# Per-head q, k and V moved by DMA in place of TensorE transposes, in a two-layer conditioned transformer block

## The chip, the cores and the metric

The program runs on one core of one Trainium2 chip. The metric is the device time of one execution in microseconds (us), lower is better. A core has five engines that run their own instruction streams and meet only at semaphores: TensorE (PE; PEld is its weight load), VectorE (DVE), ScalarE (ACT), GpSimd (POOL) and SyncE (SP), which here only issues DMAs. Sixteen DMA engines move the data. TensorE reads SBUF and writes PSUM; PSUM has 8 banks of 128 x 512 fp32.

## The reference

Inputs: x is 2 x 1024 x 288, a condition vector per batch is 288 long. Two layers follow each other.

```
U = qr(P).Q                              # 288 x 64
R = expm(skew(silu(c) W^T + b))          # one 64 x 64 rotation per batch
x = x + (x U R - x U) U^T

ada = silu(c) @ ada_w + ada_b            # six vectors of 288 per batch
h   = modulate(layernorm(x))
q, k, v = h @ qkv_w + qkv_b              # 16 heads of 18 for each token
a   = softmax(q k^T / sqrt(18)) v        # over the heads of one token, see below
x   = x + gate * (a @ proj_w + proj_b)
x   = x + gate * mlp(modulate(layernorm(x)))     # 288 -> 1152 -> gelu -> 288
```

The einsum of the attention is `nthd,ntkd->nthk`: the softmax runs over the 16 heads of one token, so every token has its own 16 x 16 score matrix. The kernel computes 8 tokens at once in one 128 x 128 matmul (8 tokens x 16 heads on each side) and masks the pairs of different tokens with extra operand rows.

## The kernel before, in words

All work is on 16 tiles of 128 tokens, handled as 4 chunks of 4 tiles. The order is written out by hand in five blocks, one per engine, with explicit semaphores. Nothing is scheduled by a planner.

1. From 0 to 111 us: the QR and the matrix exponential, a long chain of small fp32 matmuls. The weights come in and POOL splits them into fp16 halves.
2. From 111 to 217 us, the **qkv stage**: the rotation of x is finished (`delta`, `rotated`), the layernormed chunk is turned (`turn`, on PE), scaled and split into a high and a low fp16 half (`turn_out` on ACT, `split` on DVE), and multiplied with the qkv weights. The multiplication goes in 48 **slots** (`gu` 0 to 47): slots 3t, 3t+1 and 3t+2 make q, k and v of one tile. Two tiles are a **pair** (8 pairs), so a pair has 6 slots. One slot is 7 matmuls (`qkv`), a copy out of PSUM that makes the high half (`high`, ACT) and a second one that makes the low half (`low`, DVE).
3. Attention reads q and k with the head dimension on partitions. So in the qkv stage there are also **jobs**: `job` is 8 matmuls against an identity (L787 for q and k, L764 through `v_columns` for v), and `job_out` copies 128 x 512 out of PSUM on ACT (L1101, L1099) into `QKT` and `VT`. A pair has 4 jobs for q, 4 for k and 4 for v. The v jobs of pairs 4 to 7 are done later, inside the attention (`v_late`, `v_late_out`). The jobs of a slot lag the pair's products by 7 slots, so eight q and k jobs of the last pair come behind slot 47.
4. From slot 24 on, `maxima` (PE, L751) and `maximum` (DVE, L1373) compute the negative row maximum of each of the 32 **units** (64 tokens each, two 128 x 512 banks). Units 0 to 15 are done in the qkv stage, two of every three slots, units 16 to 31 in the first half of the attention. The maxima are turned by PE (`max_turn`) and written by small DMAs into one row of `QKT` (`max_row`).
5. From 217 to 282 us, the **attention**, 32 units in a software pipeline: `scores` (PE, L843), `exponentials` (ACT, L1129), `values` (PE, L880). Four units are a **round** (one pair): in each round V is regrouped by 32 small matmuls (`v_groups`, L866), copied by ACT (`v_out`, L1138) into `VG`, the output is copied out (`values_out`), turned back (`turn_values`, L896) and divided by the row sum (`normalise`, DVE). Scores of units up to 18 use one pair of banks; later ones alternate between two, since the maxima are then finished.
6. From 282 us: projection, then the MLP, which ends the program.

The PSUM banks in the qkv stage are 2 and 5 for the products (`UB`), 6 and 7 for the jobs (`CB`), 3 and 4 for the maxima, 0 and 1 for `turn`. The product of slot gu waits until the low half of slot gu - 2 is out.

The functions that the change touches follow with the line numbers of the profile.

## Time and profile before

| | us |
|---|---|
| median of 3 runs | 427.33 |
| lowest, highest | 426.06, 427.52 |
| span of the profiled execution | 422.3 |
| qkv stage | 111.0 to 217.3 |
| attention | 217.3 to 281.8 |
| projection | 281.8 to 306.6 |
| MLP | 306.6 to 422.3 |

The profile has the span of the profiled execution and no time of its own for it. The timed runs are 3.8 to 5.2 us longer than the span, and this part lies outside what the engines' records show. The stage borders are read from the first and last instruction of the lines named above. Busy time of PE is not PE at its peak: matmuls overlap, and a line's mean duration (294 ns for one of the seven matmuls of a slot) is more than twice the distance between two of them.

### The profile page before, as it was taken

How to read it: one execution, taken by the hardware profiler on the slowest of the kernel's cores; microseconds unless marked ns; L12 is line 12 of the kernel's file. 1: busy time of each engine (PE TensorE's matmuls, PEld its weight loads, DVE VectorE, ACT ScalarE, POOL GpSimd, SP SyncE). 2: the span in 40 equal slices, each digit the busy share in tenths (PEclk: the TensorE clock that was granted, in tenths of full speed). 3: DMA queues.
4: the chain of work that ended last, by engine and by line, in shares of the span. 5: the costliest groups of instructions: out<-in, count | busy, mean ns of one | idle time of the engine just before them, and what ended most of it. 6: DMA issues, size and time to landing. Idle time of an engine off the chain costs nothing.

```text
span 422.3 us, 11278 instructions
## 1 busy us (share of the span) xinstructions
PE 397.1 (94%) x4547; PEld 256.5 (61%) x4547; DVE 291.1 (69%) x793; ACT 231.8 (55%) x485; POOL 115.9 (27%) x137
## 2 busy tenths in 40 slices
PE   8999999999989899899978898889999999999996
PEld 4656555666545566666646565558755566666675
DVE  2688875677689856667757766666899776746452
ACT  3356334433257899997786785665775342422100
POOL 5039999981008700000000000005420010101040
PEclk9999989999989999999999999999999999999999
DMA  6999000000000000000000000000000000000011
GB/s 166 305 316 271 24 4 2 12 7 2 2 0 2 2 2 3 2 2 5 2 4 3 5 4 4 4 2 2 0 2 1 16 28 16 23 20 16 29 43 42
DMA packets 7926, 14.68 MB, mean 35 GB/s; under 512 B 2555, under 2 KB 6239, under 8 KB 7748
## 3 DMA queue, kind: packets, MB, share of 16 engines
q1 hardware_dynamic: 7874, 13.96, 11.0%
q8 instruction: 36, 0.59, 0.6%
q14 instruction: 16, 0.13, 0.1%
HBM read 11.52 MB, written 2.38 MB: 33 GB/s over the span
## 4 chain that ended last, share of the span: by engine, by line
PE 71%; DVE 14%; ACT 10%; issue 4%; ACTq 0%; DVEq 0%
PE psum L957 13%; PE psum L973 13%; PE psum L517 9%; PE psum L803 6%; ACT scratch L1068 3%; PE psum L787 2%; PE psum L880 2%; PE psum L617 2%; DVE MX L1373 2%; ACT big L1101 2%; PE psum L934 2%; PE psum L629 2%; PE psum L751 2%; PE psum L573 2%; PE psum L608 2%
## 5 line engine op out<-in xcount | busy, mean ns | idle before, releaser
L957 PE MATMUL psum<-scratch,W 128*128 128x512 f16 (+1 forms) x252 | 57.9, 379 | 0.0
L973 PE MATMUL psum<-W,big 128*128 128x288 f16 x432 | 55.1, 286 | 0.0
L506 POOL TENSOR_TENSOR X<-X,big 128x288 f32<-128x288 f32 x16 | 13.0, 826 | 150.0 <-ACT big L1174 149.7
L803 PE MATMUL psum<-WQ,scratch 128*128 128x288 f16 (+1 forms) x336 | 50.5, 294 | 2.8 <-DVE scratch L1368 1.9
L1199 ACT ACTIVATE big<-psum 128x512 f32<-128x512 f32 x36 | 21.3, 597 | 57.3 <-PE psum L957 52.3
L973 PEld LDWEIGHTS psum<-W,big 128*128 128x128 f16 x432 | 42.2, 98 | 12.9
L1373 DVE TENSOR_REDUCE MX<-psum 128x8 f32<-128x1024 f32 x32 | 39.0, 1220 | 11.4 <-PE psum L751 11.0
L517 PE MATMUL psum<-ident 128*32 128x192 f32 (+3 forms) x142 | 43.8, 393 | 0.0
L1129 ACT ACTIVATE big<-psum 128x1024 f32<-128x1024 f32 x32 | 32.9, 1032 | 15.0 <-PE psum L843 14.7
L957 PEld LDWEIGHTS psum<-scratch,W 128*128 128x128 f16 (+1 forms) x252 | 24.6, 98 | 25.6
L803 PEld LDWEIGHTS psum<-WQ,scratch 128*128 128x128 f16 (+1 forms) x336 | 30.6, 100 | 14.8 <-DVE scratch L1368 2.4
L1068 ACT ACTIVATE scratch<-psum,MOD 128x512 f32<-128x512 f32 (+3 forms) x48 | 34.3, 774 | 5.3 <-PE psum L728 4.0
L511 POOL TENSOR_TENSOR X<-X,scratch 128x288 f32<-128x288 f32 x16 | 13.5, 856 | 83.6 <-DVE big L1529 83.6
L1101 ACT CAST big<-psum 128x512 f16<-128x512 f32 x64 | 34.5, 597 | 0.1
L1027 ACT ACTIVATE scratch<-psum,scratch 64x65 f32<-64x65 f32 x63 | 19.5, 309 | 26.8 <-DVE scratch L1271 26.7
L1527 DVE TENSOR_SCALAR big<-big 128x512 f16<-128x512 f32 x36 | 15.6, 435 | 26.8 <-ACT big L1199 26.8
L1024 ACT ACTIVATE scratch<-scratch 64x1 f32<-64x1 f32 x63 | 12.8, 202 | 26.7 <-DVE scratch L1266 26.1
L1529 DVE SCALAR_TENSOR_TENSOR big<-big 128x512 f16<-128x512 f32 x36 | 26.3, 732 | 1.2
L1368 DVE TENSOR_TENSOR scratch<-scratch 128x512 f16<-128x512 f32 (+1 forms) x24 | 17.5, 731 | 11.1 <-ACT scratch L1068 10.9
L787 PE MATMUL psum<-ident,stage 128*64 128x128 f16 x512 | 22.2, 223 | 3.2 <-ACT big L1101 2.4
L1085 ACT ACTIVATE stage<-psum 128x576 f16<-128x576 f32 x32 | 21.0, 655 | 7.1 <-PE psum L803 6.5
L880 PE MATMUL psum<-big,scratch 128*32 128x128 f32 x512 | 22.4, 287 | 1.7 <-ACT big L1129 1.1
(221 smaller groups left out, 770.5 us busy)
## 6 DMA issues: line engine op xcount, KB each, us to landing
X<-in_x_dram SPq DMA_DIRECT2D x4, 576.0 KB, 14.8
out_dram<-big SPq DMA_DIRECT2D x16, 144.0 KB, 1.7
big<-in_L_cond_W_dram SPq DMA_DIRECT2D x1, 2268.0 KB
big<-in_L_cond_ada_w_dram SPq DMA_DIRECT2D x2, 864.0 KB, 18.2
stage<-in_L_cond_fc_w_dram SPq DMA_DIRECT2D x1, 1296.0 KB, 18.9
big<-in_L_cond_fc_w_dram SPq DMA_DIRECT2D x1, 1152.0 KB
stage<-in_L_cond_qkv_w_dram SPq DMA_DIRECT2D x1, 864.0 KB
big<-in_L_cond_fc_w_dram SPq DMA_DIRECT2D x3, 144.0 KB
```

The lines of the kernel that those rows point to most:

```text
L517: pe.matmul(out[:, 0:cols], left, left[:, 0:1].broadcast_to([P, cols]), start=True, stop=True)
L787: mm = pe.matmul(out[R * c_:R * c_ + R, P * hh:P * hh + P], HQ[:, 2 * (pr % 2) + c_, w, 4 * q + hh, :], ident16[:, :], start=True, stop=True)
L803: mm = pe.matmul(UB[gu % 2][:, 0:D], HT[0:r, n % 2, a_, P * a:P * a + P], WQ[0:r, w_, D * w:D * w + D], start=(p_ == 0), stop=(p_ == 6))
L880: mm = pe.matmul(PO[c_][32 * g:32 * g + 32, P * q:P * q + P], VG[:, w % 2, c_, 4 * q + g, :], E[:, s_ % 2, c_, P * g:P * g + P], start=Tru ...
L957: mm = pe.matmul(FB[idx % 3], W1[0:r, w_, P * m:P * m + P], HT[0:r, n % 2, a_, :], start=(p_ == 0), stop=(p_ == 6))
L973: mm = pe.matmul(YB[t % 2][:, 0:D], g[:, a_, f, cols], W2[:, w_, f, :], start=(f == 0 and a_ + w_ == 0), stop=(f == NF - 1 and w_ == 1))
L1068: act.activation(dst, src, ACT.Identity, scale=MOD[0:rows, 2 * l + 1, b, batch:batch + 1], bias=MOD[0:rows, 2 * l, b, batch:batch + 1]).th ...
L1101: act.copy(columns(QKT[pr // 4][:, w, :], 16 * (pr % 4), q), src.rearrange("p (h v m) -> p h v m", h=4, v=16)).then_inc(col_done, 1)
L1129: act.activation(E[:, s_ % 2, :, :], psum[:, 3:5, :] if s_ > PAIRED and s_ % 2 else psum[:, 0:2, :], ACT.Exp, scale=DH ** -0.5 / (QSCALE * ...
L1199: act.activation(G32[:, idx % 2, :], FB[idx % 3], ACT.Gelu, scale=1.0 / (FINE * FINE)).then_inc(gelu_sb, 1)
L1373: dve.tensor_reduce(MX[:, n, :].rearrange("p (c g) -> p c g", c=2)[:, :, 4 * u:4 * u + 4], psum[:, 3:5, :].rearrange("p a (g c) -> p a g c ...
L1529: dve.scalar_tensor_tensor(out=GT[c_ % 2][:, 1, m, :], in0=G32[:, idx % 2, :], scalar=FINE, in1=GT[c_ % 2][:, 0, m, :], op0=ALU.mult, op1= ...
```

## The change

- **q and k.** The high and low halves of a pair are written by ACT and DVE into `HQ`, now laid out so that one row holds, for each head, the 64 columns of both tiles (e) side by side. One DMA transpose for q and one for k (`turn_heads`, 128 x 2048 fp16 each) writes `QKT`. Two pairs of `HQ` are held. The 64 q and k jobs of PE and ACT are gone. The order of tokens and heads inside a pair's columns changes, and `operand` reads them with a stride; `order` is dropped, and `TOK` is built to suit.
- **V.** ACT scales v out of PSUM in fp32 (`SV`, 4 buffers). A DMA stores it in DRAM (`store_values`), 16 heads of 18 values per token, 72 bytes each at 16 places. Two DMAs per pair (`spread_values`) read it back in the grouped form `VG`, again in runs of 72 bytes. `VG` has 6 buffers; pairs 6 and 7 are read in the attention. `v_columns`, `v_groups`, `v_out`, `v_late`, `v_late_out` and the low half of v are gone.
- **Products** use three banks (`UB`), and the product of slot gu waits for slot gu - 3.
- **Maxima.** ACT scales `MX` into `MRT` without a turn on PE; four DMAs in place of two write a quarter of the pairs' row.
- **POOL** clears `VG` (128 x 4096 before the folding of the projection weights, 128 x 2048 after the last split); DVE did a smaller clear before.
- New waits: `high` of pair p waits for both transposes of pair p - 2, the v copy for the store four tiles earlier, `maxima` of a pair's first unit for its transposes, `values` for the reads of its pair.

```diff
-        HQ = stage[:, 0:4096].bitcast(F16).rearrange("p (a w h c) -> p a w h c", a=TPC, w=2, h=H)
+        SV = scratch[:, o:o + 4 * D].rearrange("p (a d) -> p a d", a=4)
+        HQ = stage[:, 0:4096].bitcast(F16).rearrange("p (a w h e c) -> p a w h e c", a=2, w=2, h=H, e=2)
...
-        UB, CB = [bank[2], bank[5]], [bank[6], bank[7]]
+        UB = [bank[2], bank[5], bank[6]]
...
+            def store_values(pr, c_):
+                k = 2 * pr + c_
+                sp.wait_ge(v_copied, k + 1)
+                sp.dma_start(values_d[pr, c_].rearrange("h p d -> p h d"), SV[:, k % 4, :].rearrange("p (h d) -> p h d", h=H)).then_inc(v_stored[k % 4], 16)
+
+            def turn_heads(pr, w):
+                if pr == NCH and w == 0:
+                    sp.wait_ge(x_rot, NT)
+                    sp.wait_ge(folded, 2 * B)
+                sp.wait_ge(qk_low, lows(6 * pr + 3 + w))
+                dst = QKT[pr // NCH][:, w, 16 * P * (pr % NCH):16 * P * (pr % NCH + 1)]
+                sp.dma_start_transpose(dst.rearrange("p (h t) -> p h t", h=H),
+                                       HQ[:, pr % 2, w].rearrange("p h e c -> p (h e c)")).then_inc(qk_in[pr], 16)
+
+            def spread_values(w):
+                for c_ in range(2):
+                    sp.wait_ge(v_stored[(2 * w + c_) % 4], 16 * (w // 2 + 1))
+                if w < 6:
+                    sp.wait_ge(vg_clear, 2 if w < 4 else 4)
+                else:
+                    sp.wait_ge(pv_ready, 4 * (w - 6) + 4)
+                for c_ in range(2):
+                    src = bass.AP(tensor=values_d.tensor, offset=values_d.offset + P * D * (2 * w + c_), ap=[[D, P], [DH, 16], [1, DH]])
+                    sp.dma_start(VG[w % 6][:, c_, :, 0:DH], src).then_inc(v_in[w], 16)
...
+            for pr in range(2 * NCH):
+                store_values(pr, 0)
+                turn_heads(pr, 0)
+                turn_heads(pr, 1)
+                store_values(pr, 1)
+                if 1 <= pr < 5:
+                    spread_values(pr - 1)
+                if pr == 6:
+                    max_row(0)
+            spread_values(4)
+            spread_values(5)
+            for n in range(1, 3):
+                max_row(n)
+                spread_values(5 + n)
+            max_row(3)
...
-                if gu >= 2:
-                    pe.wait_ge(qk_low, gu - 1)
+                if gu >= 3 and w == 2:
+                    pe.wait_ge(v_copied, gu // 3)
+                elif gu >= 3:
+                    pe.wait_ge(qk_low, lows(gu - 3))
...
-                for i in slots.get(gu, ()):
-                    job(i)
...
+                if w == 2:
+                    k = gu // 3
+                    if k >= 4:
+                        act.wait_ge(v_stored[k % 4], 16 * (k // 4))
+                    act.mul(SV[:, k % 4, :], UB[gu % 3][:, 0:D], 1.0 / (FINE * FINE)).then_inc(v_copied, 1)
+                    return
...
+                if pr >= 2:
+                    act.wait_ge(qk_in[pr - 2], 32)
```

Three places show what moves. On PE, the last slots of the qkv stage and the start of the attention, before. L803 is a slot's product, L787 are q and k jobs, L751 maxima, L757 the turn of the maxima, L843 scores, L866 the regrouping of V.

```order
L751 MATMUL psum<-big 128x128 x8
L803 MATMUL psum<-WQ,scratch 128x288 x7
L787 MATMUL psum<-ident,stage 64x128 x16
L751 MATMUL psum<-big 128x128 x8
L803 MATMUL psum<-WQ,scratch 128x288 x7
L757 MATMUL psum<-ident,MX 64x128
L787 MATMUL psum<-ident,stage 64x128 x64
L843 MATMUL psum<-big 128x128 x8
L866 MATMUL psum<-SELV,big 128x18 x32
```

The same place in the changed kernel (L800 is the product, L782 the maxima, L838 the scores, L852 the values).

```order
L782 MATMUL psum<-big 128x128 x8
L800 MATMUL psum<-WQ,scratch 128x288 x7
L782 MATMUL psum<-big 128x128 x8
L800 MATMUL psum<-WQ,scratch 128x288 x7
L838 MATMUL psum<-big 128x128 x8
L782 MATMUL psum<-big 128x128 x8
L838 MATMUL psum<-big 128x128 x8
```

The jobs between the slots, the 64 matmuls of eight jobs behind the last slot, and the regrouping of V have left PE; the scores follow the last product directly.

On ACT at the same place, before. L1080 and L1085 are `high` for v and for q or k, L1101 the job copies, L1092 the scaled maxima, L1129 the exponentials.

```order
L1101 CAST big<-psum 128x4x16x8 x2
L1085 ACTIVATE stage<-psum 128x16x36
L1101 CAST big<-psum 128x4x16x8 x2
L1080 ACTIVATE scratch<-psum 128x16x18
L1092 ACTIVATE MRT<-psum 64x128
L1101 CAST big<-psum 128x4x16x8 x8
L1129 ACTIVATE big<-psum 128x1024
```

And in the changed kernel (L1037 is the v copy, L1045 `high` for q or k, L1052 the scaled maxima, L1080 the exponentials).

```order
L1045 ACTIVATE stage<-psum 128x16x2x18
L1045 ACTIVATE stage<-psum 128x16x36
L1037 ACTIVATE scratch<-psum 128x288
L1052 ACTIVATE MRT<-MX 128x64
L1080 ACTIVATE big<-psum 128x1024 x5
```

ACT loses every job copy between the slots and the eight behind the last one.

On SP, the changed kernel's transfers of pair 4 and of pairs 6 and 7 (L377 stores V, L385 transposes q and k, L397 reads V, L405 writes the row of maxima); SP had two small transfers of maxima in this stretch before.

```order
L377 DMA value_rows<-scratch 128x16x18 [waits v_copied]
L385 DMA_TRANSPOSE big<-stage 128x16x128 [waits qk_low,folded,x_rot]
L385 DMA_TRANSPOSE big<-stage 128x16x128 [waits qk_low]
L377 DMA value_rows<-scratch 128x16x18 [waits v_copied]
L397 DMA big<-value_rows 128x16x18 [waits vg_clear,v_stored3,v_stored2]
L397 DMA big<-value_rows 128x16x18
...
L405 DMA big<-MRT 1x128x16 [waits mr_ready]
L405 DMA big<-MRT 1x128x16 x3
L377 DMA value_rows<-scratch 128x16x18 [waits v_copied]
L385 DMA_TRANSPOSE big<-stage 128x16x128 [waits qk_low] x2
```

All of it is in one queue and in order, so a transfer that waits holds back those behind it.

## Rows read from the trace of the kernel before

**Rows 1.** The page: the span.

```profile
span 422.3 us, 11278 instructions
```

**Rows 2.** Windows of qkv stage: stretch, length, busy us PE, PEld, DVE, ACT, POOL; clock.

```profile
136.20:169.60 33.40, 31.53 (x437) 21.23 (x438) 23.34 (x65) 30.62 (x61) 8.85 (x10) 1.00 0.01 2
169.60:217.30 47.70, 43.30 (x657) 29.83 (x655) 32.76 (x45) 40.57 (x79) 0.00 (x0) 1.00 0.01 3
```

**Rows 3.** Timeline, slot 24 and a slot near 188 us: start, us, engine, line.

```profile
168.05 1.03 PE L803 MATMUL psum<-WQ,scratch 128*128 128x288 f16 x7
...
187.97 1.03 PE L803 MATMUL psum<-WQ,scratch 128*128 128x288 f16 x7
188.94 0.64 PE L787 MATMUL psum<-ident,stage 128*64 128x128 f16 x16
189.05 0.65 ACT L1085 ACTIVATE stage<-psum 128x576 f16<-128x576 f32 x1
189.73 0.46 DVE L1414 SCALAR_TENSOR_TENSOR stage<-psum,stage 128x288 f16<-128x288 f32 x1 [1.31 <-ACT stage L1085]
```

**Rows 4.** Timeline: the last slot, what follows it, and the first scores.

```profile
211.08 0.40 PE L751 MATMUL psum<-big 62*128 62x128 f16 x8
211.30 0.46 DVE L1414 SCALAR_TENSOR_TENSOR stage<-psum,stage 128x288 f16<-128x288 f32 x1 [0.27 <-ACT stage L1085]
211.41 1.03 PE L803 MATMUL psum<-WQ,scratch 128*128 128x288 f16 x7
211.67 1.22 DVE L1373 TENSOR_REDUCE MX<-psum 128x8 f32<-128x1024 f32 x1
...
213.69 4.36 ACT L1101 CAST big<-psum 128x512 f16<-128x512 f32 x8
...
217.35 0.40 PE L843 MATMUL psum<-big 63*128 63x128 f16 x8
```

**Rows 5.** The page's costliest groups: the split of a turned block on DVE.

```profile
L1368 DVE TENSOR_TENSOR scratch<-scratch 128x512 f16<-128x512 f32 (+1 forms) x24 | 17.5, 731 | 11.1 <-ACT scratch L1068 10.9
```

**Rows 6.** Timeline of POOL ahead of the folding of the projection weights.

```profile
110.55 1.10 POOL L484 MEMSET scratch<- 32x512 f16 x2 [14.17 <-PE psum L685]
127.52 1.40 POOL L490 TENSOR_TENSOR big<-big 128x576 f32<-128x576 f32 x1 [15.87 <-ACT big L993]
```

**Rows 7.** DMA alone, 60 to 64 us, a store in 64 B runs: packets, MB, share of 16 engines.

```profile
q1 hardware_dynamic: 266, 0.02, 4.3%
```

**Rows 8.** DMA alone, 194 to 198 us, two 8 KB transfers in 256 B runs.

```profile
q1 hardware_dynamic: 96, 0.02, 2.1%
```

**Rows 9.** DMA alone, 340 to 346 us, one 144 KB store in 1152 B runs.

```profile
q1 hardware_dynamic: 144, 0.15, 6.9%
```

**Rows 10.** Timeline of DVE in the attention's first half: reductions of units 24 to 28.

```profile
234.23 1.23 DVE L1373 TENSOR_REDUCE MX<-psum 128x8 f32<-128x1024 f32 x1 [0.58 <-PE psum L751]
235.95 1.23 DVE L1373 TENSOR_REDUCE MX<-psum 128x8 f32<-128x1024 f32 x1 [0.50 <-PE psum L751]
237.90 1.23 DVE L1373 TENSOR_REDUCE MX<-psum 128x8 f32<-128x1024 f32 x1 [0.72 <-PE psum L751]
240.38 1.22 DVE L1373 TENSOR_REDUCE MX<-psum 128x8 f32<-128x1024 f32 x1
242.18 1.23 DVE L1373 TENSOR_REDUCE MX<-psum 128x8 f32<-128x1024 f32 x1 [0.58 <-PE psum L751]
```

**Rows 11.** Timeline of PE in the second half: scores of units 24, 28 and 31.

```profile
265.21 0.40 PE L843 MATMUL psum<-big 63*128 63x128 f16 x8
...
272.89 0.40 PE L843 MATMUL psum<-big 63*128 63x128 f16 x8
...
277.56 0.40 PE L843 MATMUL psum<-big 63*128 63x128 f16 x8
```

**Rows 12.** The chain of waits: the first slot's seven matmuls.

```profile
121.13 1.88 PE psum L803 x7
```

**Rows 13.** Window of the first slots, columns as in rows 2.

```profile
121.00:124.00 3.00, 2.87 (x13) 1.76 (x14) 2.42 (x7) 1.33 (x3) 0.00 (x0) 0.50 0.00 0
```

More of the change, by code:

```diff
@@ L143, in build @@
         T32 = scratch[:, o:o + 2 * CH].rearrange("p (a n) -> p a n", a=2)
-        VG = scratch[:, 0:4 * CH].rearrange("p (a c g d) -> p a c g d", a=2, c=2, g=16)
+        VGS = [big[:, 8192 + 2 * CH * i:8192 + 2 * CH * (i + 1)] for i in range(4)] + [scratch[:, 2 * CH * i:2 * CH * (i + 1)] for i in range(2)]
+        VG = [v.rearrange("p (c g d) -> p c g d", c=2, g=16) for v in VGS]
         o += 2 * CH
@@ L201, in build @@
         att_const = sem("att_const")
-        col_ready, col_done = sem("col_ready"), sem("col_done")
-        vcol_ready, vcol_done = sem("vcol_ready"), sem("vcol_done")
-        mr_psum, mr_ready = sem("mr_psum"), sem("mr_ready")
+        qk_in = [sem(f"qk_in{i}") for i in range(2 * NCH)]
+        v_copied = sem("v_copied")
+        v_stored = [sem(f"v_stored{i}") for i in range(4)]
+        v_in = [sem(f"v_in{i}") for i in range(2 * NCH)]
+        mr_ready = sem("mr_ready")
         max_in = [sem(f"max_in{i}") for i in range(NCH)]
@@ L297, in build @@
         MROWS = HALVES + 8
-        jobs, slots = [], {}
-        for pr in range(2 * NCH):
-            for k in range(12 if pr < NCH else 8):
-                slots.setdefault(6 * pr + 7 + k // 2, []).append(len(jobs))
-                jobs.append((pr, k // 4, k % 4))
-            for n in (0, 1):
-                if pr == (4, 6)[n]:
-                    slots.setdefault((36, 48)[n], []).append(len(jobs))
-                    jobs.append(("max", n))
-        JOB = {j: i for i, j in enumerate(jobs)}
         AHEAD = {24 + 3 * s_ // 2: s_ for s_ in range(16)}
         LATER = {st: 1 for st in range(16)}
-        ROWS_LATER, ROWS_BANK = {8: 2, 16: 3}, {8: VB[0], 16: MXB[0]}
+        ROWS_EARLY = {36: 0, 3 * 4 * NCH: 1}
+        ROWS_LATER = {8: 2, 16: 3}
         PAIRED = 18
@@ L314, in build @@
         EXP_TABLE_AT = 2 * NQ + 1
-        NSLOT = 6 * 2 * NCH + 7 + 4
-        assert max(slots) < NSLOT
+        NSLOT = NQ * NCH + 1
         def unit(gu):
@@ L393, in _ @@
-            for n in range(NCH):
+                    for k in range(2):
+                        at = 16 * P * (2 * (n % 2) + k)
+                        row = QKT[n // 2][R * c_ + MROWS:R * c_ + MROWS + 1, 0, at:at + 16 * P]
+                        sp.dma_start(row, MRT[:, n % 2, 32 * c_ + 16 * k:32 * c_ + 16 * k + 16]).then_inc(max_in[n], 16)
+            for pr in range(2 * NCH):
[7 more added lines that the diff above has]
+                    max_row(0)
@@ L441, in _ @@
                                      pattern=[[0, 1]], channel_multiplier=1))
-            chain(pool.tensor_copy(SELV[:, :], ident[:, 0:DH]))
-            for j in (DH, R, R + DH):
-                chain(pool.tensor_tensor(SELV[:, :], SELV[:, :], ident[:, j:j + DH], ALU.add))
             for src, dst, n, s_ in ((SWQ, WQ, 3 * D, in_wq), (SW1, W1, MLP, in_w1)):
@@ L726, in turn @@
                             pe.wait_ge(xn_ready, modulated(n) + 1)
-                        if n < NCH:
-                            mm = pe.transpose(f[0:rows, cols], XN[:, n % 2, j, r0:r0 + rows], order[:, :])
-                            continue
                         if not attended:
@@ L743, in maxima @@
                 if s_ % 4 == 0:
-                    pe.wait_ge(col_done, JOB[(s_ // 4, 1, 3)] + 1)
+                    pe.wait_ge(qk_in[s_ // 4], 32)
                 if s_ == 0:
@@ L1115, in _ @@
                     norm_root(1)
-                for i in slots.get(gu, ()):
-                    job_out(i)
+                if gu in ROWS_EARLY:
+                    rows_out(ROWS_EARLY[gu])
                 if GATE_AT <= gu < GATE_AT + 4:
@@ L1163, in _ @@
                         values_out(st // 4 - 1)
-                    if st % 4 < 2 and st // 4 + 1 == 4:
-                        for q in range(2 * (st % 4), 2 * (st % 4) + 2):
-                            v_late_out(st // 4 + 1, q)
-                if st % 4 == 3 and st // 4 + 1 < UNITS // 4:
-                    v_out(st // 4 + 1)
             def product_out(t):
@@ L1454, in normalise @@
                     dve.wait_ge(weights, 5)
+                    for pr in range(2 * NCH):
+                        dve.wait_ge(qk_in[pr], 32)
                 for c_ in range(2):
@@ L1483, in _ @@
                     values_out(st // 4 - 1)
-                if st % 4 < 2 and 4 < st // 4 + 1 < UNITS // 4:
-                    for q in range(2 * (st % 4), 2 * (st % 4) + 2):
-                        v_late_out(st // 4 + 1, q)
                 if st >= 4 and st % 4 == 2:
```

211 lines of the change are left out of this document (55 added, 156 removed).

## The prediction

> **What bounds the kernel now.** I read the windows by stage first, since the share of a whole span mixes stages, then the timeline inside the two stages that the change touches, then the DMA queue. The change leaves everything before 121 us and after 282 us alone, so the question is how long the 161 us between them become.
>
> In the qkv stage two windows matter [rows 2]. From 136.2 to 169.6 us (slots 8 to 24) ACT is busy 30.6 of 33.4 us and PE 31.5; DVE only 23.3. From 169.6 to 217.3 us ACT is busy 40.6 of 47.7 us, PE 43.3, DVE 32.8. The jobs fill PE and ACT. A slot's seven matmuls occupy PE for 0.97 us (187.97 to 188.94), a pair of jobs is 0.64 us more, and the job copies keep ACT so that the next thing waits [rows 3]. Behind the last slot (211.41 us) come 4.36 us of job copies, and the first scores start only at 217.35 [rows 4]. In the attention's first half the reductions of the maxima follow each other on DVE at 1.72 to 2.48 us [rows 10]; in the second half a round of four units takes 7.68 us (265.21 to 272.89) with V's matmuls and copies in it, while the last round, which has none, does three units in 4.67 us [rows 11].
>
> **Slots 8 to 24.** The jobs leave: 17 slots x 0.64 us = 10.9 us of PE, so PE keeps 31.5 - 10.9 = 20.6 us. ACT loses its job copies and drops far below. DVE loses the low half of v in 5 or 6 slots, 2.5 us by 0.46 us each [rows 3], and keeps 20.8 us [rows 2]. PE and DVE are now equal. Two engines that hand work to each other never both stay full, so I add 3 us to the floor of 20.8 and take 23.9 us for 33.4: **9.5 us less**. The ends are 12.6 (the floor) and 5.
>
> **Slots 24 to 47.** Here a round of three slots (q, k, v) with two maxima is a chain. From rows 3 and 4: product to next PE work 0.97 us, product start to `high` 1.08, `high` start to `low` 0.68, `low` holds DVE 0.37 before a maximum can start, a maximum is 1.22, maxima hold PE 0.33 (211.08 to 211.41), PE to DVE 0.45. Start the q product at 0. Its low half is on DVE at 1.76; the first maximum runs 2.13 to 3.35. The k product starts at 1.30, but the second maxima wait on PE for that first maximum until 3.40, so v's product starts at 3.73 and the next q at 4.70. A round is 4.70 us, bound by the pair PE-DVE; ACT has air. 23 slots are 7.67 rounds, 36.0 us, and three turned blocks with a 0.73 us split each [rows 5] add about 1 us each: 39.0 us. Before it took 43.4 us (168.05 to 211.41) [rows 3, 4]: **4.4 us less**. The ends are 0 and 9 (PE alone, 3 x 0.97 + 2 x 0.33 a round).
>
> **Behind slot 47.** The scores follow the product: 217.35 - 211.41 - 0.97 = **5.0 us less** [rows 4]. The clear of `VG` goes to POOL, which stood idle for 15.87 us before the folding [rows 6]: free. If it weren't, the transposes of pair 4 would wait for the folding, at slot 28, 15 us later. With these three terms the scores start 18.9 us earlier. The row of maxima goes out by four transfers in place of two, but it is asked for at slot 41 and at the last slot, and read at the first and at the ninth unit; 8 KB transfers land within 2 us of queue and engine time unless the queue is full, which is the case below.
>
> **Attention.** First half: a round of reductions is 7.95 us now (234.23 to 242.18). Without V's steps the interval 1.95 becomes 1.72, and the normalising step keeps its 2.48 [rows 10]: 7.64, times four rounds, 1.2 us less, and 0.8 for the first regrouping that stood ahead of the first maxima. Second half: the last round, with its fourth unit at the mean of the three, is 6.2 us against 7.68 [rows 11]; three rounds have V's work: 4.4 us less. Together **6.4 us less** (ends 2 and 12).
>
> **What it adds: 48 transfers on one queue.** No row shows a transpose. Prices per transfer come from packets. The store in 64 B runs took 4.3% of 16 engines x 4 us = 2.75 us for 266 packets, 10.3 ns each [rows 7]; V's 72 B runs are the nearest thing, 2048 of them over 16 engines: 1.3 us a store or a read. Transfers from SBUF to SBUF in 256 B runs took 1.34 us of engine time for 16 KB [rows 8]; a transpose reads 512 KB, 32 times as much, 43 us over 16 engines: 2.7 us. The ends: at the rate of 1152 B runs (6.6 us for 144 KB) it is 1.5 us [rows 9]; if it moves 64 B pieces it is 8192 x 10.3 ns / 16 = 5.3 us; if each piece written is 16 rows of one 2-byte column, 32 B, it is 10.5 us. I take 2.7, since those are the only SBUF to SBUF rows.
>
> Call the price of a transpose X. Pair 1 is ready at about 137 us. Pairs 1 to 4 put 2X + 5.2 us in the queue each (two transposes, two stores, two reads), pair 5 a store and two transposes before its `qk_in`, and 2 us is landing: done at 137 + 10X + 24.1 = 161.1 + 10X. Slot 42 needs it, and six slots (9.0 us) follow until the scores. So the DMA alone lets the scores start at 170.1 + 10X. At X = 2.7 this is 197.1; the engines give 217.35 - 18.9 = 198.5. The queue is just behind the engines' pace and costs nothing, but each further 0.1 us of X then costs 1 us. This is the thin place of the forecast. `high` of pair p + 2 is the waiting instruction; behind it on ACT stand the v copies and the scaling of the next chunk, and through them PE.
>
> The Trainium skill (DMA: Bandwidth & Descriptors, section Latency and other measured facts) gives 261 GB/s for a transpose with a non-contiguous middle dimension; by an estimate from that figure, 512 KB take 2.0 us, and the queue would be out of the way. The trace has no transpose to check it.
>
> **Sum.** Span 422.3 [rows 1] - 9.5 - 4.4 - 5.0 - 6.4 = 397.0 us. The page gives no time beside its span; the median of the runs, 427.3, lies 5.0 us above it. 397.0 + 5.0 = **402 us**, 6% less. Its own range is 391 to 412.
>
> **Rivals.**
>
> *The queue takes part of it.* X lies between 3.5 and 5.3 us. The scores then start at 205 to 223 us, and with 6.4 us from the attention the time is 409 to 427. For it: 64 B pieces are priced at 5.3. Against: nothing in the trace.
>
> *The queue turns it slower.* Transposes in 32 B pieces: X = 10.5. Scores start at 275.1, 57.8 us later than now; pair 7's transposes land 48.5 us after pair 5's, at 314.6, where unit 28's maxima want them at about 298, 16.5 us more; less 6.4: 427.3 + 57.8 + 16.5 - 6.4 = 495 us. It is decided by X alone: from 170.1 + 10X - 217.35 = 6.4, X = 5.4 us, the kernel is slower than before. The same holds at a smaller X if V's packets cost more than 10.3 ns: each ns more is 0.13 us on a transfer, 2.2 us over the 17 that stand between pair 1 and the transposes of pair 5. The place is ACT's wait for `qk_in`. For it: neither a transpose nor a run that scatters into DRAM at 72 B steps has been seen, and 64 B packets already move only 6 GB/s an engine against 23 for 1152 B [rows 7, 9].
>
> The Trainium skill states that against this change on the same page, section Specifications: below 512 B a DMA engine does read-modify-write and is off line rate. The trace agrees that short runs are slow; their price above includes it for aligned 64 B runs, not for 72 B ones.
>
> A second sentence there, in DMA Transpose, lets only one transposing stream run at a time; all transposes are on SP here, so it changes nothing.
>
> *TensorE falls to its lower clock.* PE is busy less: 3.57 of 4.70 us in a round. The first slots, behind a wait of PE, ran at a granted clock of 0.50, 1.2 GHz, one product taking 1.88 us for 0.97 [rows 12, 13]. If half of the eight rounds ran so, each with 3 x 0.91 us more on PE less the 1.1 us that PE has spare, it costs 4 x 1.6 = 6.5 us, 13 if all did: 408 to 415. Against it: the clock stayed at 1.00 through both windows of rows 2.
>
> *The gain is not there.* PE and DVE block each other in slots 8 to 47 as before; only the tail and the attention pay: 427.3 - 5.0 - 6.4 = 416.
>
> **How the numbers follow.** Forecast (391 to 412): 0.46. Queue takes part: 0.14. Queue turns it slower: 0.28, of which I hold half to be under 455, X being anywhere from 5.4 up. Clock: 0.06. Gain not there: 0.06. About 0.5% (2 us) is what a measurement here tells from no change. Faster by more: 0.46 + 0.06 + 0.06 and 0.11 of the second case, 0.69; within it 0.04; slower 0.27. The range for 8 in 10 starts at 390 (0.05 left below) and goes up to 462, leaving about 0.13 above.
>
> **What would show it.** Right: first scores near 198 us, last slot's product 1 us before them; a round of slots 24 to 47 near 4.7 us; ACT idle, DVE above 80% busy in slots 24 to 47; landing times of transposes under 6 us, the wait of ACT for `qk_in` near zero; rounds of 7.6 us in the attention's first half, 6.2 in the second. Wrong: ACT, and PE behind it, wait for transposes at the start of each pair, with a DMA share near 1 (engine-bound) or low (then SP's issue or the crossbar sets the pace, not packets); a granted clock of 0.5 between 140 and 197 us.

## The result, and the profile after

The changed kernel takes **460.8 us** (median of 4 runs, 454.3 to 472.8) against 427.3 us before: a ratio of 1.074, 95% interval 1.066 to 1.081. The forecast was 402 us with a range from 390 up to 462. The direction was wrong. The ratios, here and below, leave out executions in a slower state (here the one of 472.8 us, which is also the profiled one), while the medians take in all.

The page's span is 471.0 us [rows 1]. In this one execution the stage before the first product ran 13 us longer than before (134.48 for 121.13 us), though the change leaves it alone; the other three have spans of 452 to 459. So stages are compared from the first product on. Timeline of PE after: start, us, engine, line; in square brackets the idle time before, and what ended it. The lines are the first slot, the last slot, the first scores, and the first product of the projection.

```profile
134.48 0.91 PE L800 MATMUL psum<-WQ,scratch 128*128 128x288 f16 x6 [1.89 <-DVE scratch L1297]
...
227.48 1.03 PE L800 MATMUL psum<-WQ,scratch 128*128 128x288 f16 x7
...
232.84 1.16 PE L838 MATMUL psum<-big 63*128 63x128 f16 x8 [4.32 <-DMA big<-MRT]
...
334.78 3.62 PE L892 MATMUL psum<-WP,scratch 128*128 128x288 f16 x28
```

From first product to first scores it is 98.4 us, where before took 96.2 [rows 4, 12] and the forecast was 77.4. From first scores to the projection it is 101.9 us, where before took 68.7 (217.35 to 286.09) and the forecast was 62.3. So 2 us were lost in the stage that should have paid 19, and 33 in the stage that should have paid 6. The scores do not follow the last product directly either: they start 5.4 us behind it (227.48 to 232.84), of which PE waits 4.32 us for the DMA that writes the first row of maxima from `MRT` into `QKT`.

What fills the attention is seen in its timeline after (same columns). It answers to [rows 10, 11].

```profile
241.44 1.17 PE L838 MATMUL psum<-big 63*128 63x128 f16 x8
242.43 1.14 PE L782 MATMUL psum<-big 62*128 62x128 f16 x8
242.65 1.02 ACT L1080 ACTIVATE big<-psum 128x1024 f32<-128x1024 f32 x1 [2.04 <-PE psum L838]
243.49 1.08 PE L852 MATMUL psum<-big 128*32 128x128 f32 x16
244.50 1.17 PE L838 MATMUL psum<-big 63*128 63x128 f16 x8
```

A unit comes every 3.06 us, and by the records PE never pauses in it. Eight matmuls of 128 columns, scores or maxima, occupy PE for 1.0 us where they took 0.33 before. ACT waits for PE. The groups by line say it for the whole stretch. Of PE before, 121 to 300 us (busy us, mean ns of one; L880 values, L751 maxima, L843 scores, L896 the turn of the values):

```profile
L880 PE MATMUL psum<-big,scratch 128*32 128x128 f32 x512 | 22.4, 287 | 1.7 <-ACT big L1129 1.1 <-ACT scratch L1146 0.3
L751 PE MATMUL psum<-big 62*128 62x128 f16 x256 | 13.1, 223 | 3.2 <-DVE MX L1373 3.1
L843 PE MATMUL psum<-big 63*128 63x128 f16 x256 | 12.9, 220 | 2.0 <-ACT big L1129 1.8
L896 PE MATMUL psum<-ident,scratch 128*128 128x128 f32 x64 | 8.7, 278 | 1.5 <-DVE scratch L1472 0.9 <-DVE big L1476 0.5
```

And after, 134 to 345 us:

```profile
L838 PE MATMUL psum<-big 63*128 63x128 f16 x256 | 37.1, 423 | 5.1 <-DMA big<-MRT 4.3 <-ACT big L1080 0.6
L782 PE MATMUL psum<-big 62*128 62x128 f16 x256 | 36.6, 418 | 8.9 <-DVE MX L1302 8.8
L852 PE MATMUL psum<-big 128*32 128x128 f32 x384 | 24.3, 399 | 0.1
L863 PE MATMUL psum<-ident,scratch 128*128 128x128 f32 x64 | 15.6, 426 | 0.9 <-DVE scratch L1398 0.9
```

Scores and maxima took about 24 us more each. Values and their turn, whose matmuls are the same, are slower too (399 ns for 287, 426 for 278), where the granted clock was low. Windows after (busy us of PE, PEld, DVE, ACT, POOL; then granted clock, DMA share, GB/s):

```profile
200.00:210.00 10.00, 8.65 (x55) 4.96 (x55) 4.46 (x6) 2.36 (x6) 0.00 (x0) 0.75 0.85 105
...
240.00:250.00 10.00, 10.00 (x110) 5.49 (x108) 3.95 (x4) 4.76 (x6) 0.00 (x0) 0.50 0.71 63
...
310.00:320.00 10.00, 10.00 (x106) 5.82 (x104) 2.72 (x6) 4.10 (x4) 0.00 (x0) 0.50 0.00 0
```

Before, the clock was 1.00 in the qkv stage from 136 us on [rows 2], and 0.94 and 1.00 in the two halves of the attention. Now it is 0.50, the 1.2 GHz level, in the two attention windows shown and 0.60 over the whole attention, though PE is busy for 99.8 of its 101.9 us. In the qkv stage the DMA share is near 1 (0.88 over the whole stage), and `high` on ACT waits four times for transposes (us in total, times, longest):

```profile
ACT stage L1045 <- DMA big<-stage: 8.7, 4, 4.5
```

Timeline of SP after, the transposes of pairs 1, 3, 4 and 5 (pairs count from 0):

```profile
155.47 5.36 SPq L385 DMA_TRANSPOSE big<-stage  x2
...
180.70 6.64 SPq L385 DMA_TRANSPOSE big<-stage  x2
...
194.91 5.26 SPq L385 DMA_TRANSPOSE big<-stage  x2
...
207.98 6.24 SPq L385 DMA_TRANSPOSE big<-stage  x2
```

Pairs follow each other at 13 us; my queue was 10.6 a pair (2 x 2.7 + 5.2). A store of V by itself, 139 to 142.5 us, answers to [rows 7]:

```profile
q1 hardware_dynamic: 2064, 0.15, 37.7%
```

37.7% of 16 engines x 3.5 us is 21.1 us for 2064 packets, 10.2 ns each, as priced. The error in the queue is not in the price of a store that has the queue to itself.

### The profile page after: what moved, and what is told of

It reads as the page before. It is cut to its first block, busy times and chain, and to the rows that moved or that the text cites. A ratio compares the mean times of both kernels' runs of the same rounds, so it can differ in the third digit from the quotient of the medians.

```text
span 471.0 us, 9049 instructions
## 1 busy us (share of the span) xinstructions
PE 442.5 (94%) x3519; PEld 271.4 (58%) x3519; DVE 276.0 (59%) x763; ACT 187.1 (40%) x385; POOL 120.1 (25%) x135
## 4 chain that ended last, share of the span: by engine, by line
PE 80%; DVE 8%; DMA 5%; ACT 4%; issue 2%; SPq 1%; ACTq 0%; DVEq 0%
PE psum L915 12%; PE psum L931 11%; PE psum L551 10%; PE psum L838 7%; PE psum L852 6%; PE psum L782 5%; PE psum L800 5%; DMA big<-stage 4%; PE psum L863 3%; PE psum L651 3%; PE psum L762 2%; PE psum L663 2%; PE psum L598 2%; PE psum L892 2%; ACT scratch L1026 2%
## 5 line engine op out<-in xcount | busy, mean ns | idle before, releaser
L800 PE MATMUL psum<-WQ,scratch 128*128 128x288 f16 (+1 forms) x336 | 53.9, 314 | 5.2 <-DVE stage L1342 2.9
L1080 ACT ACTIVATE big<-psum 128x1024 f32<-128x1024 f32 x32 | 32.8, 1025 | 56.5 <-PE psum L838 56.3
L551 PE MATMUL psum<-ident 128*32 128x192 f32 (+3 forms) x142 | 48.2, 427 | 0.0
L800 PEld LDWEIGHTS psum<-WQ,scratch 128*128 128x128 f16 (+1 forms) x336 | 33.6, 106 | 24.9 <-issue 10.0
L782 PE MATMUL psum<-big 62*128 62x128 f16 x256 | 36.6, 418 | 8.9 <-DVE MX L1302 8.8
L838 PE MATMUL psum<-big 63*128 63x128 f16 x256 | 37.1, 423 | 5.1 <-DMA big<-MRT 4.3
L782 PEld LDWEIGHTS psum<-big 62*128 62x128 f16 x256 | 17.9, 148 | 22.0 <-DVE MX L1302 11.7
L1045 ACT ACTIVATE stage<-psum 128x576 f16<-128x576 f32 x32 | 20.2, 648 | 22.6 <-PE psum L800 13.9
L838 PEld LDWEIGHTS psum<-big 63*128 63x128 f16 x256 | 16.5, 150 | 20.3 <-issue 13.8
L1342 DVE SCALAR_TENSOR_TENSOR stage<-psum,stage 128x288 f16<-128x288 f32 x32 | 14.4, 454 | 23.2 <-ACT stage L1045 23.0
```

The source lines that it names most:

```text
L551: pe.matmul(out[:, 0:cols], left, left[:, 0:1].broadcast_to([P, cols]), start=True, stop=True)
L782: mm = pe.matmul(MXB[c_][:, P * g:P * g + P], operand(s_, c_, 0, g, MROWS), operand(s_, c_, 1, g, MROWS), start=True, stop=True)
L800: mm = pe.matmul(UB[gu % 3][:, 0:D], HT[0:r, n % 2, a_, P * a:P * a + P], WQ[0:r, w_, D * w:D * w + D], start=(p_ == 0), stop=(p_ == 6))
L838: mm = pe.matmul(SB[s_ % 2 if s_ > PAIRED else 0][c_][:, P * g:P * g + P], operand(s_, c_, 1, g, MROWS + 1), operand(s_, c_, 0, g, MROWS + ...
L1045: act.mul(dst[:, :, 0:2, :] if w else dst[:, :, 0:3:2, :], src.unsqueeze(2).broadcast_to([P, H, 2, DH]), QSCALE / (FINE * FINE)).then_inc( ...
L1080: act.activation(E[:, s_ % 2, :, :], psum[:, 3:5, :] if s_ > PAIRED and s_ % 2 else psum[:, 0:2, :], ACT.Exp, scale=DH ** -0.5 / (QSCALE * ...
```

## The experiments

Three theories. *Stride*: `operand` now picks its 128 columns 16 apart, 32 B in fp16, and TensorE reads such an operand slowly. *Queue*: transposes and V's packets set the pace. *Clock*: TensorE simply falls to its lower clock, for waits or otherwise. A unit's scores, or its maxima, are eight matmuls of 128 columns, called "the eight" below; each matmul has a stationary operand (the weight load) and a moving one. The stage times of all runs stand in one table behind the experiments.

**e0_after.** No edit.

> The changed kernel again, for stage times beside the runs that follow. All theories: a span of 450 to 460 us, eight matmuls of scores or maxima about 1.1 us, qkv stage (first product to first scores) about 98 us, attention about 94 us.

Measured: 465.5 us (452.9 to 473.0, ratio to before 1.069, interval 1.056 to 1.082). The stages are those above within 0.5 us; 102.4 us for the attention is more than the 94 expected.

**e1_contig_both, e2_contig_weights, e3_contig_moving.**

```diff
-            return cols.rearrange("p (t v) -> p v t", v=16)[:, v]
+            return cols[:, P * v:P * v + P]        # both; in e2 the stationary operand alone, in e3 the moving one
```

> Leaves the computation of the reference: both operands of scores and maxima are 128 neighbouring columns of one head, in place of 16 heads x 8 tokens taken 16 columns apart; everything else as changed. Theory stride (the step of 32 B in the operands makes these matmuls slow): eight matmuls fall from 1.1 to 0.33 to 0.40 us, an attention round of four units from 12.3 to about 8 us, the time to 415 to 430 us. Theory queue (the transposes and V's transfers set the time): the matmuls may fall, but qkv stays at 98 us and the kernel above 445 us. Theory clock (TensorE runs at its lower clock there whatever it reads): eight matmuls stay above 0.75 us in the attention and the time above 445 us.

> Leaves the computation of the reference: only the stationary operand (the weight load) of scores and maxima is 128 neighbouring columns; the moving one keeps its step of 16 columns. Stride theory, if the weight load is what is slow: eight matmuls 0.4 us. If the moving side is: they stay at 1.1 us. If both are: 0.6 to 0.9 us. Queue and clock theories: time within 2% of the changed kernel.

> Leaves the computation of the reference: only the moving operand of scores and maxima is 128 neighbouring columns; the weights keep their step of 16 columns. Stride theory, if the moving side is what is slow: eight matmuls 0.4 us. If the weight load is: they stay near 1.1 us. If both: 0.6 to 0.9 us. Queue and clock theories: time within 2% of the changed kernel.

Measured: both 426.8 us (ratio 0.999, 0.995 to 1.004), weights alone 453.4 (1.064, 1.050 to 1.077), moving alone 429.3 (1.002, 0.998 to 1.007). The stride costs 34 us by the medians and 32 by the ratios, and it is the moving operand that is slow: by itself contiguous it gives back nearly all of it. Groups of PE with the moving operand contiguous (e3), 110 to 460 us:

```profile
L784 PE MATMUL psum<-big 62*128 62x128 f16 x256 | 16.6, 259 | 20.3 <-DVE MX L1304 20.2
L840 PE MATMUL psum<-big 63*128 63x128 f16 x256 | 16.2, 252 | 12.4 <-DMA big<-MRT 9.2 <-ACT big L1082 3.1
```

With the weights alone contiguous (e2):

```profile
L784 PE MATMUL psum<-big 62*128 62x128 f16 x256 | 35.1, 405 | 13.7 <-DVE MX L1304 13.7
L840 PE MATMUL psum<-big 63*128 63x128 f16 x256 | 34.8, 403 | 4.1 <-DMA big<-MRT 3.6 <-ACT big L1082 0.2
```

All the gain is in the attention (101.9 to 65.4 and 68.2 us). The qkv stage stays at 98 to 104 us, so something else sets it. The clock theory, by which the time would have stayed above 445 us whatever is read, falls here: the granted clock over the attention follows the moving operand, 0.60 in the changed kernel, 0.67 in e2, 0.89 in e3 and 0.93 in e1.

The 104.0 us of e1 need a correction. In its profiled execution the clock was 0.56 from 121 to 130 us and 0.71 from 130 to 140, where e3 had 0.82 and 1.00; the product of slot 5 starts 14.6 us behind the first in place of 10.3 (at 135.86 and 131.12 us). The profiled executions of f1, i1, f4 and h1 below have the same longer low stretch (0.50 to 0.55 until 130 us), those of e2, f2, i2, g1 and g2 have not (0.81 to 0.86). The edits do not explain it, since both groups have runs of the same form (f1 and i1 in one, f2 and i2 in the other). It puts about 4 us on the first stage time of e1, f1 and i1. The 109.8 of f4 and the 103.6 of h1 begin with such a stretch too.

**f4_before_strided.** The same edit the other way round, on the kernel before.

```diff
-            return QKT[b][R * c_:R * c_ + rows, w, P * (4 * u + g):P * (4 * u + g + 1)]
+            pr, v = divmod(4 * u + g, 16)
+            cols = QKT[b][R * c_:R * c_ + rows, w, 16 * P * pr:16 * P * (pr + 1)]
+            return cols.rearrange("p (t v) -> p v t", v=16)[:, v]
```

> The kernel before, no DMA transposes and V by PE; only operand reads scores' and maxima's columns 16 apart (the tokens are then mixed, so it leaves the computation of the reference). Theory stride: eight matmuls 1.1 us for 0.33 to 0.40, 64 groups by 0.7 us is 45 us of PE, a part of it hidden: 455 to 475 us. Theory that the transposes or their DMA traffic slow PE's reads of SBUF: no change, 425 to 432 us.

Measured: 476.3 us (1.112, 1.106 to 1.118), 48 us more by the ratio, at the upper end of what was expected. The stride alone does it, without transposes or V's transfers beside it. Its timeline of PE at a granted clock of 1.00 (L845 scores, L882 values):

```profile
307.43 1.12 PE L845 MATMUL psum<-big 63*128 63x128 f16 x8
308.49 0.64 PE L882 MATMUL psum<-big,scratch 128*32 128x128 f32 x16
```

The strided eight take 1.06 us to the next work at clock 1.00, and 0.99 to 1.07 at 0.50 (241.44 to 242.43 and 242.43 to 243.49 above for scores and maxima): their time hardly depends on the clock, while the values' goes from 0.57 to 1.01. And its window over 32 strided groups, columns as above:

```profile
229.60:286.50 56.90, 56.53 (x713) 34.78 (x711) 23.46 (x28) 25.16 (x37) 0.00 (x0) 0.61 0.01 2
```

PE is busy 56.5 of 56.9 us by the records, waits for other engines are nearly nil (0.4 us), and still the granted clock is 0.61. So the clock falls behind the strided matmuls, not behind waits, and the low clock is a second cost of the stride. The strided matmuls do not always bring it: from 300 to 312 us of the same run, with V's unstrided matmuls between the scores and PE busy for 11.7 of 12 us, it is 1.00. What decides between the two was not followed up.

**h1_steps.** The step measured by itself on the kernel before; the unit's number sets it.

```diff
+            k = (1, 2, 4, 8, 16, 0)[s_ % 6]
+            if k == 0 and moving:
+                return cols.rearrange("p (h v m) -> p v h m", h=16, v=16)[:, v]
+            k = max(k, 1)
+            return cols[:, 0:P * k].rearrange("p (t v) -> p v t", v=k)[:, v % k]
```

> A measurement on the kernel before (leaves the computation of the reference): the operands of scores and maxima of unit s are 128 columns at a step of 1, 2, 4, 8 or 16 columns (2 to 32 B) by s mod 6, and for s mod 6 = 5 the moving operand is 16 runs of 8 neighbouring columns, 256 B apart. If the step makes the read slow in proportion up to some size: eight matmuls 0.33 to 0.40 us at step 1 and 2, 0.6 at 4, 1.1 from 8 or 16 on. If any step over one column does it: 1.1 us at 2, 4, 8 and 16. Runs of 8: 0.4 us in either case, if reads within a run stay whole. Whole time between before's 427 and 465 us.

Measured (442.98 us, one run), scores of units 18 to 23 at clock 1.00: steps of 1, 2, 4, 8, 16 columns, then 16 runs of 8.

```profile
269.01 0.40 PE L849 MATMUL psum<-big 63*128 63x128 f16 x8
271.43 0.40 PE L849 MATMUL psum<-big 63*128 63x128 f16 x8
273.05 0.64 PE L849 MATMUL psum<-big 63*128 63x128 f16 x8
274.75 1.13 PE L849 MATMUL psum<-big 63*128 63x128 f16 x8
277.30 1.15 PE L849 MATMUL psum<-big 63*128 63x128 f16 x8
279.97 0.40 PE L849 MATMUL psum<-big 63*128 63x128 f16 x8
```

By these records steps of 2 and 4 B are free, 8 B costs 1.6 times, 16 B and 32 B the same 2.8 times, and runs of 16 B, 256 B apart, cost nothing. By the distance to the next work of PE it is 0.33, 0.33, 0.57, 1.06, 1.08 and 0.33 us. That is the first of the two expectations. In units with a step both operands have it; that the moving one carries the cost is known from e2 and e3, at 32 B. What fits all six is that the number of elements in one 16 B piece counts. The Trainium skill says so (Advanced Engine Details and Errata, section Memory Cachelines: SBUF has lines of 16 bytes, at least two hits on a line are needed, a new line at each access is penalised). The trace agrees with the penalty; at two hits a line (the step of 8 B) it is already 1.6 times, where by the Trainium skill it would be free. I had not weighed this in the prediction, and it speaks against the very layout that the change brings in.

**f1_few_values, f2_few_transposes, i1_few_stores, i2_few_reads.** All start from e1_contig_both, so that the stride is out, and take away traffic with the number of DMAs kept. The lines are shortened.

```diff
-  sp.dma_start(values_d[pr, c_].rearrange("h p d -> p h d"), SV[...].rearrange("p (h d) -> p h d", h=H))
+  sp.dma_start(values_d[pr, c_].rearrange("h p d -> p h d")[:, 0:1], SV[...].rearrange(...)[:, 0:1])   # f1, i1
-  src = bass.AP(..., ap=[[D, P], [DH, 16], [1, DH]])
-  sp.dma_start(VG[w % 6][:, c_, :, 0:DH], src)
+  src = bass.AP(..., ap=[[DH, P], [DH, 1], [1, DH]])                                                   # f1, i2
+  sp.dma_start(VG[w % 6][:, c_, 0:1, 0:DH], src)                                                       # f1, i2
+  src = bass.AP(..., ap=[[DH, P], [0, 16], [1, DH]])                                                   # i1
-  sp.dma_start_transpose(dst.rearrange("p (h t) -> p h t", h=H), HQ[:, pr % 2, w]...)
+  sp.dma_start_transpose(dst.rearrange("p (h t) -> p h t", h=H)[:, 0:2], HQ[:, pr % 2, w, 0:2]...)     # f2
-  return cols[:, P * v:P * v + P]
+  return cols[:, P * (v % 2):P * (v % 2) + P]                                                          # f2
```

> Leaves the computation of the reference, as e1_contig_both does (neighbouring columns), and of V only one head's 18 values per token are stored and read back: a sixteenth of V's packets, the number of DMAs unchanged. Compare with e1_contig_both (427 us, qkv stage 104 us from first product to first scores). Theory queue: a pair's 13 us of queue fall to two transposes, the engines' pace of about 4.7 us a round sets the stage, which ends 16 to 24 us sooner: 403 to 411 us. Theory engines (PE and DVE block each other, the queue only looks full): less than 5 us, above 422 us. Theory transposes (each takes over 4.5 us by itself): 5 to 12 us, the DMA share between them still near 1.

> Leaves the computation of the reference: as e1_contig_both, but a transpose turns two of the sixteen heads, and all scores and maxima read these two; V's transfers whole. Compare with e1_contig_both (427 us). Theory queue with V's packets as the larger part: V's 5.2 us or more a pair are below the engines' 9.4 us, so the stage ends 16 to 24 us sooner, 403 to 411 us. If the V packets by themselves cost 10 us or more a pair, less than 12 us is gained. Theory engines: above 422 us.

> Leaves the computation of the reference: as e1_contig_both (427 us), the reads of V whole (the same 2048 runs of 72 B each), the stores cut to one head, a sixteenth of their packets. With few V packets at all it was 399 to 401 us. If reads cost 2.7 us each of 16 engines and stores 1.3 (sum over both measured about 4 us): a pair needs 2 x 3.0 + 2 x 2.7 = 11.4 us of queue, more than the engines' 9.4: 409 to 418 us. If both cost 2.0: 401 to 408 us.

> Leaves the computation of the reference: as e1_contig_both (427 us), the stores of V whole, the reads cut to one group, a sixteenth of their packets. If stores cost 1.3 us each: a pair needs 8.6 us of queue, under the engines' 9.4: 399 to 404 us. If stores and reads both cost 2.0: 401 to 408 us, the same as i1_few_stores. If the scattering stores are the dear ones (2.7): 409 to 418 us.

The reads of i1 are whole in number and size, but fetch one head's 72 B of each token sixteen times, not sixteen different runs.

Measured: f1 399.4 us (0.934, 0.932 to 0.937), f2 403.3 (0.944, 0.941 to 0.947), i1 402.8 (0.945, 0.939 to 0.950), i2 410.5 (0.961, 0.952 to 0.970), against 426.8 with all traffic. f2 lies in the range of the queue theory, f1 4 us below it, and both are far from the engines' 422. The queue costs 27 us, and taking away any part of it gives back 16 to 27. With a sixteenth of V's packets or an eighth of the transposes the engines set the pace. Timeline of DVE in f2, every third `low`:

```profile
184.38 0.45 DVE L1342 SCALAR_TENSOR_TENSOR stage<-psum,stage 128x288 f16<-128x288 f32 x1
...
188.97 0.45 DVE L1342 SCALAR_TENSOR_TENSOR stage<-psum,stage 128x288 f16<-128x288 f32 x1
...
193.56 0.45 DVE L1342 SCALAR_TENSOR_TENSOR stage<-psum,stage 128x288 f16<-128x288 f32 x1
...
198.16 0.45 DVE L1342 SCALAR_TENSOR_TENSOR stage<-psum,stage 128x288 f16<-128x288 f32 x1
```

A round is 4.59 us; the forecast's chain gave 4.70. A pair, two rounds, is 9.2 us of engines.

Of the cases set out for i1 and i2, the one with dear reads (i1 at 409 to 418 us) fell, and the one with dear scattering stores (i2 at 409 to 418) came true: the stores cost more than the reads. The queue's totals, 121 to 260 us (packets, MB, share of 16 engines; 139 us times the share is the time), with all traffic (e1):

```profile
q1 hardware_dynamic: 101056, 13.16, 78.1%
```

with few values (f1):

```profile
q1 hardware_dynamic: 40192, 8.75, 37.9%
```

with few stores (i1):

```profile
q1 hardware_dynamic: 70912, 10.97, 54.7%
```

and with few reads (i2):

```profile
q1 hardware_dynamic: 70912, 10.97, 71.0%
```

That is 108.6, 52.7, 76.0 and 98.7 us. The transposes are 52.7 / 16 = 3.3 us each, at most, with the small transfers counted in. Reads add 23.3 us, 1.55 each (15 whole reads' worth of packets). Stores add 46.0, 3.1 each, though one by itself took 1.3 above. Reads and stores together add 55.9, less than the sum of both. The same window of g1_values_only, the run below that moves V whole and has no transpose at all:

```profile
q1 hardware_dynamic: 66432, 4.79, 37.1%
```

This is 51.6 us for 16 stores, 16 reads and the small transfers, 1.6 each. So the packets' time is no fixed price: beside transposes and without the reads a store adds 2.3 times what it took alone, and V's transfers among themselves are already above 1.3. Whether beside transposes the store's packets or the transposes' grow was not told apart; for pairs 2 to 6 two transposes hold SP 7.4 to 8.9 us in i2 where in i1 they hold it 4.4 to 5.5.

**g1_values_only, g2_early_jobs.** The half of the change that the two causes spare: on the kernel before, V goes through DRAM, and PE still turns q and k, so nothing is strided for PE and no transpose is queued.

```diff
-            for k in range(12 if pr < NCH else 8):
+            for k in range(8):
...
-                    act.copy(columns(QKT[pr // 4][:, w, :], 16 * (pr % 4), q), src.rearrange("p (h v m) -> p h v m", h=4, v=16))
+                act.copy(columns(QKT[pr // 4][:, w, :], 16 * (pr % 4), q), src.rearrange("p (h m v) -> p h v m", h=4, v=16))
...
+                    act.mul(SV[:, k % 4, :], UB[gu % 2][:, 0:D], 1.0 / (FINE * FINE)).then_inc(v_copied, 1)
+            (store_values, spread_values, VG and its clear as in the changed kernel)
```

> The reference's computation in full. q and k by PE's jobs as in the kernel before; only V goes through DRAM as in the changed kernel (stores, reads, six buffers of VG, cleared by POOL), natural order of tokens, put right when ACT copies q and k out of PSUM. Theory queue and stride: without transposes the queue has 5.2 us of work a pair in 15 us and costs nothing, the operands are contiguous; gain 4 to 8 us in the attention and 3 to 8 in the qkv stage: 410 to 421 us, faster than both. Rival: V's short packets land so late, or ACT's PSUM reads 64 B apart are so slow, that nothing is left: 427 us or more.

> The reference's computation in full. As g1_values_only (413.8 us), but with V's jobs gone the q and k jobs of a pair stand two slots earlier (5 to 8 slots behind the pair's first product in place of 7 to 10), so six of them are left behind the last slot in place of eight. If the tail behind the last product is on the path: 1 to 2 us less, 411.5 to 413. Rival: a job so close behind its low half makes PE wait in every pair: no change or 1 to 4 us more.

Measured: g1 **413.8 us** (0.969, 0.964 to 0.974), faster than both kernels. g2 417.5 us (0.979, 0.971 to 0.987), a gain that is not clear of 2%. Its rival came true: the tail behind the last product is 0.6 us shorter, but the slots before it are 5.4 us longer. PE's waits for maxima on DVE grew from 2.6 to 5.7 us there; how the earlier jobs bring that about was not followed up, and each stage time is from one execution. Timeline of PE in g1, first slot, last slot, first scores, projection:

```profile
121.05 3.40 PE L829 MATMUL psum<-WQ,scratch 128*128 128x288 f16 x14 [1.89 <-DVE scratch L1338]
...
205.64 1.03 PE L829 MATMUL psum<-WQ,scratch 128*128 128x288 f16 x7
...
212.00 0.61 PE L869 MATMUL psum<-big 63*128 63x128 f16 x8
...
275.29 3.62 PE L928 MATMUL psum<-WP,scratch 128*128 128x288 f16 x28
```

Stages of all profiled runs, us, read from lines like these:

| run | median | first product to first scores | first scores to projection |
|---|---|---|---|
| forecast | 402 | 77.4 | 62.3 |
| before | 427.3 | 96.2 | 68.7 |
| after | 460.8 | 98.4 | 101.9 |
| e0 (after again) | 465.5 | 98.1 | 102.4 |
| e2 (weights contiguous) | 453.4 | 99.1 | 93.0 |
| e3 (moving contiguous) | 429.3 | 98.1 | 68.2 |
| e1 (both) | 426.8 | 104.0 (about 4 of it the early low clock) | 65.4 |
| i2 (e1, few reads) | 410.5 | 87.1 | 62.2 |
| f2 (e1, few transposes) | 403.3 | 81.4 | 62.1 |
| i1 (e1, few stores) | 402.8 | 81.9 (the same) | 61.7 |
| f1 (e1, few values) | 399.4 | 82.4 (the same) | 62.9 |
| f4 (before, strided) | 476.3 | 109.8 | 105.9 |
| h1 (before, steps of 1 to 16) | 443.0 | 103.6 | 81.1 |
| g1 (before, values by DRAM) | 413.8 | 91.0 | 63.3 |
| g2 (g1, jobs earlier) | 417.5 | 95.8 | 63.0 |

## Why the prediction was wrong

**The step that failed is in "Slots 24 to 47": "maxima hold PE 0.33 (211.08 to 211.41)", and with it the unchanged scores in "Attention".** The number was read from a kernel whose operands are 128 neighbouring columns [rows 4, 11], and carried over to one whose operands lie 32 B apart. The description of the change names the stride; no term and no rival priced it. It is 1.0 to 1.06 us in place of 0.33, in 64 groups. It sets the sign by itself: without it the whole change comes out at 427 us, no change, in spite of the queue. The range reached up to 462 us and so holds the 460.8, but by luck: its upper part was there for transposes of X = 5.4 us and more, and they cost at most 3.3.

**The clock** had 0.06 and a bill of 6.5 to 13 us, argued from idle time of PE in the qkv stage. Behind idle time it did fall in the qkv stage (in e3 to 0.80 and 0.86 from 160 to 180 and from 180 to 200 us, with PE busy for 12.2 and 13.7 of 20 us), but there the queue set the pace. The large part came where PE is never idle, by the stride. Its part there can be estimated from a round of the attention's second half. f2 makes it in 5.9 us (240.53 to 246.39 by its scores) at clock 1.00; after in 10.3 (302.83 to 313.10) at 0.50. At full clock, strided scores and values would be 4 x (1.06 + 0.57) + 1.0 for the turn, 7.5 us: by this estimate 1.7 us of the 4.4 are the strided matmuls' own time, 2.7 the lower clock of the others.

**The queue.** The place was named rightly ("the thin place of the forecast", ACT's wait for `qk_in`, a DMA share near 1), the sizes were too low in both terms: transposes up to 3.3 us for X = 2.7, V's transfers (108.6 - 52.7) / 30 = 1.9 for 1.3. By the forecast's own formula 170.1 + 10 x 3.3 + 17 x 0.6 is 213.3 for the first scores. With the moving operand contiguous (e3) the last product ended at 213.9, but the scores came at 218.9:

```profile
212.93 1.03 PE L802 MATMUL psum<-WQ,scratch 128*128 128x288 f16 x7
218.91 0.65 PE L840 MATMUL psum<-big 63*128 63x128 f16 x8 [4.95 <-DMA big<-MRT]
```

The rest is a wait that the formula does not have, for the first row of maxima. Its four DMAs were issued only at 213.16 us, since they stand in the queue behind the transposes of pair 6, which held SP from 203.76 to 212.50. So "Behind slot 47", 5.0 us less, failed as well: the scores start 5.4 us (after), 6.0 (e3) and 7.0 (e1) behind the start of the last product, where before took 5.9 and the forecast 1.0. It came true where the queue was light: 1.0 us in f1 and i1. The price of this row was put at nothing "unless the queue is full", and the rival with the full queue did not count it. So the rival "the queue takes part" was true in kind, beside a cause that was not on the list; X stayed just under its 3.5, V's transfers and the row of maxima made up the rest, and the 16 to 27 us that a lighter queue gives back (i2 to f1) are its price. The 64 B row that I took for V had been a transfer with an empty queue beside it. The 261 GB/s that the Trainium skill states for a transpose (DMA: Bandwidth & Descriptors, section Latency and other measured facts) would make 2.0 us, an estimate; by the queue's totals one took up to 3.3 us here, and no run shows one by itself.

**Right, once the two are out.** The round, 4.59 us for 4.70. The qkv stage of the engines alone, 81.4 to 82.4 us for 77.4: the excess is about 4 us of early low clock in f1 and i1, and in f2 the row of maxima (2.8 us), so without these it is 77.8 to 78.6. The attention, 61.7 to 62.9 us for 62.3, with rounds in f2 of 7.4 to 7.8 us (7.64) in the first half and 5.9 (6.2) in the second. f1, 399.4 us, comes closest to the forecast's kernel, and 402 was its forecast. POOL's clear of `VG` cost nothing visible, as said.

**Slips in the sums.** The end of 9 us for slots 24 to 47 does not follow from its condition: PE alone, 3.57 us a round, makes 7.67 x 3.57 + 3 = 30.4 us, 13 less than before. And the 5.0 us by which the median lies above the span are not all outside the records: in every run with both numbers the time is 1.7 to 1.9 us above the span of the same execution, and the rest is that the profiled execution of before was a short one. Neither moves the 402.

Sum for after: 402 + 21.0 (98.4 for 77.4) + 39.6 (101.9 for 62.3) = 462.6, measured 460.8.

## What to carry to other kernels

A duration from the trace belongs to its access pattern as well as to its shape: when a change alters the layout that an untouched instruction reads, that instruction is part of the change and needs a price, on the moving operand of TensorE above all. Keep 16 B together there (8 fp16 values): runs of 16 B cost nothing here at 256 B apart, the one distance that was tried. Look also at what else of the program comes out of the same queue, such as a small row that the next stage waits for. And when a queue comes out just under the engines' pace, its transfers will be in flight together, and here lone transfers priced them too low.

## What was not expected of the hardware

- fp16 operands at steps of 2 and 4 B read at full rate, at 8 B 1.6 times as long, at 16 and 32 B 2.8 times (0.40, 0.40, 0.64, 1.13, 1.15 us for eight matmuls of 128 columns); at 32 B it is the moving operand that costs. A stationary operand at 32 B steps cost little: 259 and 252 ns mean in e3 against 244 and 233 in e1.
- The strided read takes nearly the same time at either clock (1.06 us at 1.00, 0.99 to 1.07 at 0.50), and the granted clock fell to 0.50 and 0.61 behind such matmuls with PE busy for over 99% of the stretch. A full busy share of PE in the profile is no sign that the clock holds.
- 72 B packets that scatter into DRAM: 10.2 ns each for a store alone, 1.3 us; 1.6 us a transfer with only V's stores and reads in the queue; 3.1 us added by a store beside transposes.
- ACT's copy out of PSUM at steps of 16 values (g1) takes 1.07 us for two, as the copies before did without that step, so nothing of g1's gain was lost there.
